# Eight loads of one attention unit move from SyncE's instruction stream to ScalarE's

## The reference

```python
qkv = x @ qkv_w.T
q, k, v = jnp.split(qkv, 3, axis=-1)
...
q = _apply_rot(q, cos, sin)
k = _apply_rot(k, cos, sin)
...
outs.append(_sdpa(q[:, :N1], k[:, :N1], v[:, :N1], 1.0 / math.sqrt(HD)))
outs.append(_hyp_attn(q[:, N1:N1 + N2], k[:, N1:N1 + N2], v[:, N1:N1 + N2], curvature))
...
outs.append(_sdpa(qn, kn, v[:, N1 + N2:], math.sqrt(HD)))
```

## Time and profile before

| | us |
|---|---|
| median of three runs | 2944.15 (2942.97 to 2952.62) |
| the profiled execution | 2938.4 |
| its span, first to last instruction | 2935.6 |

### The profile page before, as it was taken

One profiled execution on the slowest core, in us unless ns is written; L12 is line 12 of the kernel. 1 busy time (PEld: TensorE's weight loads), 2 busy tenths in 40 slices (PEclk: granted clock), 3 DMA queues, 4 the chain that ended last, 5 costly groups with the idle time before them and its releaser, 6 DMA issues. The chain is left out here.

```text
span 2935.6 us, 30082 instructions
## 1 busy us (share of the span) xinstructions
PE 2281.7 (78%) x10649; PEld 858.5 (29%) x10649; DVE 1614.4 (55%) x3381; ACT 1380.2 (47%) x1963; POOL 664.3 (23%) x639
## 2 busy tenths in 40 slices
PE   3798857777999884777798986677779988577779
PEld 1232321223433341122343333122333324212134
DVE  2553446677456354675655535467655534466662
ACT  1145315893234531787224442379513453158932
POOL 1012101332321210332231120133233121023324
PEclk9699866678999985777899987678889998666789
DMA  5100220001400022000320013110041002200012
GB/s 141 41 18 2 73 72 29 17 1 49 126 26 18 16 68 76 30 2 1 104 89 25 2 44 79 37 32 1 11 131 52 18 1 73 72 30 17 1 35 88
DMA packets 67749, 128.31 MB, mean 44 GB/s; under 512 B 11300, under 2 KB 24740, under 8 KB 62980
## 3 DMA queue, kind: packets, MB, share of 16 engines
q1 hardware_dynamic: 67600, 126.40, 14.8%
HBM read 109.99 MB, written 15.20 MB: 43 GB/s over the span
## 5 line engine op out<-in xcount | busy, mean ns | idle before, releaser
L1278 DVE TENSOR_REDUCE mx<-ps 128x1 f32<-128x512 f32 (+3 forms) x1248 | 643.6, 553 | 545.6 <-PE ps L628 448.0
L1007 ACT ACTIVATE pr<-ps 128x1024 f32<-128x1024 f32 (+3 forms) x672 | 516.2, 805 | 523.8 <-PE ps L698 521.5
L625 PE MATMUL ps<-kop,qop 72*128 72x512 bf16 (+6 forms) x1248 | 435.2, 368 | 157.3 <-DVE mx L1278 89.9
L698 PE MATMUL ps<-qop,kop 75*128 75x512 bf16 (+7 forms) x1344 | 406.3, 366 | 162.5 <-DMA kop<-parts_scratch 56.3
L744 PE MATMUL ps<-pr,vt 128*32 128x512 f32 (+3 forms) x2688 | 434.6, 579 | 5.6 <-POOL pr L1543 4.8
L1543 POOL TENSOR_SCALAR_AFFINE_SELECT pr<-pr 128x512 f32<-128x512 f32 x224 | 147.4, 658 | 969.3 <-ACT pr L1007 967.9
L1062 ACT ACTIVATE pr<-ps 128x512 f32<-128x512 f32 x224 | 133.8, 598 | 408.8 <-PE ps L850 320.0
L625 PEld LDWEIGHTS ps<-kop,qop 72*128 72x128 bf16 (+1 forms) x1248 | 123.6, 100 | 602.7 <-DVE mx L1278 340.7
L860 PE MATMUL ps<-pr,w_down 128*128 128x512 f32 x384 | 211.5, 638 | 71.4 <-POOL pr L1534 50.4
L698 PEld LDWEIGHTS ps<-qop,kop 75*128 75x128 bf16 (+1 forms) x1344 | 121.8, 104 | 379.0 <-ACT pr L1007 124.6
L847 PE MATMUL ps<-hT,w_gate 128*128 128x512 f32 x384 | 205.6, 618 | 8.2 <-DVE on L1481 8.1
(11 more groups left out here) (287 smaller groups left out, 3048.2 us busy)
## 6 DMA issues: line engine op xcount, KB each, us to landing
wb<-gates_scratch SPq DMA_DIRECT2D x192, 256.0 KB, 3.4
qop<-parts_scratch SPq DMA_DIRECT2D x96, 192.0 KB
kop<-parts_scratch SPq DMA_DIRECT2D x96, 192.0 KB
on<-hmax_scratch SPq DMA_DIRECT2D x8, 1024.0 KB, 5.6
parts_scratch<-on SPq DMA_DIRECT2D x24, 256.0 KB, 3.4
parts_scratch<-wb SPq DMA_DIRECT2D x24, 256.0 KB, 2.9
xin<-in_x SPq DMA_DIRECT2D x4, 512.0 KB, 4.5
on<-in_cos SPq DMA_DIRECT2D x4, 512.0 KB, 3.8
```

The lines of the kernel that those rows point to most:

```text
L625: mm = pe.matmul(o, qop[0:k, slot(l, u), j, qb * P:(qb + 1) * P], kop[0:k, slot(l, u), j, k0:k0 + wd], start=True, stop=not diag)
L698: mm = pe.matmul(o, kop[0:k, slot(l, u), 2 * pair + j, kb * P:(kb + 1) * P], qop[0:k, slot(l, u), 2 * pair + j, q0:q0 + wd], start=True, s ...
L1007: nc.scalar.activation(pr[:, g % 3, 2 * pair:2 * pair + 2, o0:o0 + wd], ps[:, bank:bank + 2, o0:o0 + wd], ACT.Exp).then_inc(a.exps, 1)
L1278: ins_ = nc.vector.tensor_reduce(mx[:, nth(l, u) % 2, j, qb, col % 2:col % 2 + 1], ps[:, bank, 0:wd], AX.X, ALU.max, negate=True)
```

## The change

`load_rows` and `load_unit` move out of SP's program and take the issuing engine as an argument. In layer 1, SP issues the loads of units 0 and 1 and leaves out those of the hyperbolic unit. ACT issues these eight behind `prepare()` and ahead of `attention(1)`, after two waits for the six stores. Layer 0's loads, and those of unit 2, stay where they were.

```diff
+        def load_rows(queue, l, u, side, i):
+            op = (qop, kop)[side]
+            heads = scratch[l, side, :, :, 4 * u:4 * u + 4, :].rearrange("i d h n -> i d (h n)")
+            if side:
+                src = heads[i:i + 1].broadcast_to([3, HD, 4 * N])
+            else:
+                src = heads.rearrange("i d n -> (i d) n")
+            queue.dma_start(op[24 * i:24 * i + 24, slot(l, u), :, :].rearrange("p h n -> p (h n)"),
+                         src).then_inc(at[l].ops[u], 16)
+
+        def load_unit(queue, l, u):
+            a = at[l]
+            for side in range(2):
+                if u == 0:
+                    queue.wait_ge(a.stored[side], 48)
+                for i in range(3):
+                    load_rows(queue, l, u, side, i)
+            if is_hyp(l, u):
+                for op, rows, ready in ((qop, trow[0], t_row), (kop, trow[1], t_krow)):
+                    queue.wait_ge(ready, 1)
+                    queue.dma_start(op[TROW:TROW + 9, slot(l, u), :, :], rows).then_inc(a.ops[u], 16)
...
             prepare()
+            for side in range(2):
+                act.wait_ge(at[1].stored[side], 48)
+            load_unit(act, 1, HYP_UNIT)
             attention(1)
...
-            for u in (0, HYP_UNIT, 1):
-                load_unit(1, u)
+            for u in (0, 1):
+                load_unit(sp, 1, u)
```

More of the change, by code:

```diff
@@ L1599, in sync_program @@
         def sync_program(sp, b):
[L1600 to L1622, removed]
             def store_parts(l, side, first, p):
@@ L1654, in operands0 @@
                 store_parts(0, 0, 3, parts0[:, 0])
-                load_unit(0, 0)
+                load_unit(sp, 0, 0)
                 for n in range(12):
                     yield LOADS_FROM + n
-                    load_rows(0, 1 + n // 6, n // 3 % 2, n % 3)
+                    load_rows(sp, 0, 1 + n // 6, n // 3 % 2, n % 3)
             def send_maxima(l, more, u, chunks):
@@ L1700, in sync_program @@
             sp.wait_ge(at[0].pv, NS)
-            load_unit(0, 3)
+            load_unit(sp, 0, 3)
             for u in (2, 3):
@@ L1717, in sync_program @@
             sp.wait_ge(at[1].pv, NS)
-            load_unit(1, 2)
+            load_unit(sp, 1, 2)
             send_maxima(1, b + 1 < B, 2, BOTH)
```

## The result

The changed kernel takes 2980.24 us (median of 4 runs, 2974.77 to 2984.52) against 2944.73 for the kernel before in the same comparison. The medians are 35.5 us apart. The ratio is 1.0109, with a 95% interval of 1.0088 to 1.0129, and it is not the quotient of the medians: by it the change costs 32 us (26 to 38). The forecast was 2963, slower, range 2944 to 2980. The direction and the place are right. The median is 0.24 us past the range's upper end; the ratio times the 2944.15 from which the forecast started is 2976, inside it. The size is 1.7 to 1.9 times what I had worked out (19 us).

A forecast was written before the change was run, and what follows sets the result against it. Bound: TensorE waiting for operand loads at layer 1's attention start, `kop` loads on three engines, in four sequences. Sum 0 + 0 + 4 x 4.8 = +19 us on 2938.4, plus 5.75 for the median: 2963; range 2944 to 2980.

The forecast's parts named there:

- SP's eight issues at 0: Layer 1's start: SP loses eight issues, 5.3 us, so unit 1's loads are issued sooner; nobody gains, worth 0.
- ACT's issues at 0: ACT before its first layer-1 exponential: two waits and eight issues, 5.3 us, covered by 14.43 us of idle time; worth 0.
- Turns between the two queues: Layer 1's operand loads: the three engines serve SP's and ACT's queues alternately, row by row, half each.
- Rival 1: Late queue served last: unit 1's loads pass ahead of the hyperbolic `kop` loads, piece 8.3 us later, 2977; chance 0.12.
- Rival 3: Two queues keep the three engines fuller in the slow stretch up to 418 us: faster, 2940 or 2934; chance 0.09.
- The signs that I had named: Trace after, layer 1's start: scores at 425 to 426, wait 19 to 20 us, shorter piece wait, piece at 435 to 438.
- The 4.8 us that count: Hyperbolic unit's first piece, each sequence: 364 kB of unit 1 served ahead of it, 436.0 for 431.17; four times, +19 us.
- by the time it is through, the hyperbolic unit has had 422 as well: Equal shares from 408: while unit 0's last 422 kB load, the hyperbolic unit gets 422 kB, leaving it 364.
- My ledger: Sequence 0's kB on the three engines: unit 0 737, hyperbolic unit 786, unit 1 737; 31 kB/us before 418, 76 after.
- the small packets: Rows of `tq` and `tk`, 2 KB, alternating with unit 1's 8 KB rows: 1.9 us more, kept for the range.
- The bound from above, 8.3: Most the first piece can move, with all of unit 1's traffic ahead: 439.5 - 431.17 = 8.3 us.
- the equal share: Two queues get half each of the three engines; 4.8 us chosen as nearest to this, between bounds 0 and 8.3.

The follow-up runs named there:

- the second experiment: Changed kernel, but SP issues unit 1's six layer-1 loads only when all of the hyperbolic unit's have landed; ratio 0.9974 to the kernel before.
- the swapped roles: Changed kernel, but ACT issues unit 1's loads and SP those of unit 0 and the hyperbolic unit; ratio 1.0138 to the kernel before.
- the new row order: Kernel before with contraction rows feature outermost, copy innermost, in `qop` and `kop`, both layers, so loads' outer dimension is 8; 2876.02 us, ratio 0.974.

## Why the prediction came out as it did

*SP's eight issues at 0*: right. Unit 1's loads are issued earlier, and nothing gains.

*ACT's issues at 0*: right. They took 5.5 us for the 5.3 of SP's rows, began some 1 us earlier than I had said, beside the copy, and ended 13 us ahead of the exponential. In the second experiment they are all there, and the kernel is no slower than before.

*Turns between the two queues*: right, and shown by the packet counts, by the kernel with unit 1 held back, and by the swapped roles. Rival 1, service in the order of issue, had the better number (2977). But its mechanism is refuted by the delay of the first scores, 4.0 us where it has none, and by the equal counts. My range reached 2980 only because of this rival, so that the result lies at its edge and not clearly outside is luck.

*Rival 3, a fuller use of the engines*: refuted. From 414 to 424 the changed kernel's window shows 111 GB/s for 107 in the earlier trace rows, and 76 for 76 after it. Within it the two queues do move more for a while (141 GB/s from 416 to 420, where one queue reached 123), but less afterwards, and the traffic ends no earlier.

*The signs that I had named*: mixed. Counted from ACT's copy at 405.69, the first scores come at 423.7 for the 425 to 426 forecast, after a wait of 18.1 us on average for 19 to 20. The wait at the first piece was to be shorter and is longer, 12.1 for 8.1. The piece comes at 438.8, just past the 435 to 438 of the forecast and nearly at the 439 that I had kept for rival 1. All four differ in one direction: unit 0 lost less, and the piece more, than I had worked out.

*The 4.8 us that count*: mis-sized, 7.9 measured. Two terms of it were too small.

First, the step "by the time it is through, the hyperbolic unit has had 422 as well". Unit 0 lost 4.0 us, not 5.5, which at 76 GB/s is 304 kB served beside it. My ledger had put too little work on the three engines before 408, by drawing one rate from 402.6 to 418. The queue moved 0.73 MB from 402.6 to 408, 135 GB/s against the 107 after it; that the three engines had their part of this is worked out, not shown. What the hyperbolic unit doesn't get beside unit 0 it gets beside unit 1: 786 - 304 = 482 kB, 6.3 us instead of 4.8.

Second, the small packets, which I had worked out at 1.9 us and kept for the range. The counts at 440 us and the kernel in which SP issues them show the effect in both directions. They belonged in the sum: 6.3 + 1.9 = 8.2. Measured 7.9. With both, the sum would have been 4 x 8.2 = 33, near the measured 32 (by the ratio) to 35.5 (by the medians).

The bound from above, 8.3, was itself too low. It was the time from the start of the piece, which by the ledger is 1.4 us behind its last byte, to the end of the traffic. The ledger's own 737 kB at 76 GB/s are 9.7 us; with unit 1 wholly ahead the piece was 9.2 and 10.3 us later in the two kernels that show it. So the changed kernel lost most of unit 1's traffic but not all, and rival 1 would have been 4 x 9.7 = 39, 2983.

I had also chosen the equal share as "nearest" between 0 and 8.3, when each correction that I had named could only push towards the ceiling: the hyperbolic loads start later than unit 0's, and their last packets are the small ones.

*The rest*: 31.8 us are in the eight waits, of 32 by the ratio or 35.5 by the medians. The profiled execution lies 46.1 us above that of before, 14 more than the waits explain. 5.9 of these are there before the first changed instruction of sequence 0, where no work differs. The granted clock of the windows differs there: 100 to 140 us stood at 0.66 before and stands at 0.54 after. The kernel before shows the same scatter by itself: in another comparison its runs lay between 2941.51 and 2967.82 us. So I take this part for noise of the clock and not the change; that is not tested. My remark that the clock did not fall back in sequence 0 holds only for the rows that I showed: it was 0.76 from 444 to 446 us and 0.50 from 446 to 452.

## What to carry to other kernels

A DMA queue served in order is a priority list, as these runs show it; a load moved to a second queue leaves it, and what was behind it is then served beside it. So before splitting loads over two issuing engines, ask which of them must land first, and whether anything less urgent is left in the other queue; holding that back behind a wait made the loss vanish. If the stretch is bound by transfers, look first at how many engines a load uses: the DMA share gives it (0.19 is three of 16), and an outer dimension of 8 for 3 was worth 2.6% where the second queue cost 1.1%.

## What the runs showed of the hardware

- Two queues on the same engines take turns by packet, not by bytes: 15 and 15 packets, 0.11 and 0.03 MB, and 15 to 18 packets for 0.02 to 0.15 MB with the roles exchanged. This is as the Trainium skill has it in "DMA: Bandwidth & Descriptors", section "Queues, rings and completion order". The packets of the large loads here are rows of 8 KB.
- Issuing from a second engine can cost time though it saves issue time. The same page's section "Issuing engines are not separate DMA queues" says that such DMAs interleave on the same 16 engines and that only the sequencer's issue time is saved. The trace agrees with the interleaving (45 and 43 packets); the ratio of 1.0109 shows that by it the time can get worse.
- Three busy engines moved 25 GB/s each (76/3) and the eight of the new row order 20 (163/8). From 408 to 418 in the earlier trace rows, with the `qop` loads, the share of 0.64 is some ten engines, which moved 10 each (107/10): an engine can be busy and slow. I had expected the limit to be on the total, at 107 to 123. 163 GB/s with the new row order, and 141 for 4 us with two queues, show that it isn't; what it is stays open.
- The number of engines follows the outer dimension of the load: 3 gave a share of 0.19, 8 gave 0.51.
